# Second layer's Hadamard transform moved from TensorE to sums on GpSimd and VectorE

## The reference, cut to what matters

```python
def _ffn_ref(x, W1, W2, W3):                 # W1, W3: 1024 x 256, W2: 256 x 1024
    up_gate = jnp.einsum('bsd,hd->bsh', x, W1)
    up_lin = jnp.einsum('bsd,hd->bsh', x, W3)
    hidden = jax.nn.silu(up_gate) * up_lin
    hidden = fwht(hidden)                    # Walsh-Hadamard transform over 1024, times 1/sqrt(1024)
    out = jnp.einsum('bsh,dh->bsd', hidden, W2)
    return out

xn = _layernorm(x)
s, g = mixing(xn), silu(_ffn_ref(xn, W1, W2, W3))
x = x + s * g
```

## Time and profile before

| What | Value |
|---|---|
| median of 3 runs (lowest to highest) | 355.48 us (355.43 to 355.82) |
| time of the profiled execution | 355.68 us |
| its span | 353.6 us |
| TensorE busy | 347.7 us (98%) |
| VectorE busy | 249.3 us (71%) |
| ScalarE busy | 170.4 us (48%) |
| GpSimd busy | 109.7 us (31%) |
| DMA queue of SP, share of 16 engines | 37.9% |

### The profile page before, as it was taken

How to read it: one execution, slowest core, us unless ns; L and a number is a source line. 1 busy time by engine, 2 the same in 40 slices (tenths; PEclk the granted TensorE clock), 3 DMA queues, 4 the chain that set the end, 5 groups by cost and what they waited for, 6 DMA issues and landing times.

```text
span 353.6 us, 4944 instructions
## 1 busy us (share of the span) xinstructions
PE 347.7 (98%) x1760; PEld 295.6 (84%) x1760; DVE 249.3 (71%) x491; ACT 170.4 (48%) x335; POOL 109.7 (31%) x125
## 2 busy tenths in 40 slices
PE   7999999999999999999999999999999999999996
PEld 4888888888888888888987788888888888888896
DVE  5679973995489667966497956788657887367624
ACT  2865442446254724354466634654346544464531
POOL 2164410456026944663026030160300703004011
PEclk9999999999999999999999999999999999999999
DMA  7999479215141303130341401436014252064001
GB/s 262 239 186 214 111 142 154 61 44 126 50 111 29 121 1 118 32 121 0 115 142 41 123 0 59 142 80 198 3 50 149 72 135 74 0 193 129 7 0 61
DMA packets 70200, 34.44 MB, mean 97 GB/s; under 512 B 41248, under 2 KB 70176, under 8 KB 70176
## 3 DMA queue, kind: packets, MB, share of 16 engines
q1 hardware_dynamic: 69760, 33.80, 37.9%
q10 hardware_dynamic: 416, 0.33, 0.3%
HBM read 21.99 MB, written 12.12 MB: 96 GB/s over the span
## 4 chain that ended last, share of the span: by engine, by line
PE 90%; DVE 4%; POOL 2%; ACT 2%; DMA 1%; issue 1%; SPq 0%; DVEq 0%; POOLq 0%; ACTq 0%
PE GU L359 18%; PE GU L360 18%; PE GU L361 18%; PE O L359 8%; PE O L360 8%; PE O L361 8%; POOL X L1267 1%; PE O L420 1%; DMA X<-in_L_attn_x 1%; PE O L504 1%; PE O L503 1%; PE O L502 1%; PE T L361 1%; PE T L360 1%; PE T L359 1%; PE T L366 1%
## 5 line engine op out<-in xcount | busy, mean ns | idle before, releaser
L717 ACT ACTIVATE hf<-GU 128x512 f32<-128x512 f32 x64 | 38.2, 599 | 79.1 <-DVE hid L845 63.0
L1001 DVE TENSOR_TENSOR hf<-hf,GU 128x512 f32<-128x512 f32 x64 | 43.5, 680 | 27.7 <-PE GU L361 22.5
L359 PE MATMUL GU<-XT,W1T 128*128 128x512 f32 x128 | 50.5, 394 | 0.0
L845 DVE TENSOR_TENSOR hid<-hf,hid 128x512 fp32r<-128x512 f32 x64 | 50.0, 783 | 0.3
L359 PE MATMUL GU<-XT,W3T 128*128 128x512 f32 x128 | 49.9, 390 | 0.0
L361 PE MATMUL GU<-XT,W1T 128*128 128x512 f32 x128 | 49.9, 390 | 0.0
L360 PE MATMUL GU<-XT,W1T 128*128 128x512 f32 x128 | 49.9, 390 | 0.0
L361 PE MATMUL GU<-XT,W3T 128*128 128x512 f32 x128 | 49.8, 389 | 0.0
L360 PE MATMUL GU<-XT,W3T 128*128 128x512 f32 x128 | 49.8, 389 | 0.0
L360 PE MATMUL O<-hid,W2hi 128*128 128x512 f32 x112 | 43.7, 390 | 0.0
L359 PE MATMUL O<-hid,W2hi 128*128 128x512 f32 x112 | 43.7, 390 | 0.0
(11 more groups left out here) (200 smaller groups left out, 725.7 us busy)
## 6 DMA issues: line engine op xcount, KB each, us to landing
swap_rows<-GX SPq DMA_DIRECT2D x7, 512.0 KB, 3.1
sT<-swap_rows SPq DMA_DIRECT2D x28, 128.0 KB, 2.7
swap_gate<-GX SPq DMA_DIRECT2D x7, 512.0 KB, 2.9
sT<-swap_gate SPq DMA_DIRECT2D x28, 128.0 KB, 2.7
stage<-in_L_ffn_W SPq DMA_DIRECT2D x12, 256.0 KB, 3.9
swap_p<-PX SPq DMA_DIRECT2D x4, 640.0 KB, 3.7
PL<-swap_p SPq DMA_DIRECT2D x16, 160.0 KB, 3.2
stage<-in_L_ffn_W SPq DMA_DIRECT2D x32, 64.0 KB, 2.6
```

The lines of the kernel that those rows point to most:

```text
L359: pe.matmul(o, lhs(0), rhs(0), start=start, stop=False)
L717: act.activation(hf[:, c % 2, :], GU[:, c % 2, 0, :], ACT.Silu).then_inc(silu_done, 1)
L845: dve.tensor_tensor(dst, src, hi_part.bitcast(F32), ALU.subtract).then_inc(done, 1)
L1001: dve.tensor_tensor(hf[:, c % 2, :], hf[:, c % 2, :], GU[:, c % 2, 1, :], ALU.mult).then_inc(mul_done, 1)
```

## The change

The transform over the 128 positions of a chunk no longer uses TensorE. It is done in seven steps of sums and differences.

- Five steps on GpSimd, on the blocks as loaded and before they are transposed, where five of the seven bits of the position lie along the free dimension: `inner_butterfly(0)` to `(9)`, two instructions a step (all sums, then all differences), each with 1024 elements a partition in runs of 16, 8, 4, 2 and 1, between U2[1] and U[1]. Numbers 0 to 4 are in group 1 and 5 to 9 in group 2.
- `turn_w2` follows, all four in group 2 (two at c = 3, two at c = 7). `pair_butterfly` and `quad_butterfly` stand in groups 2 and 3, `last_butterfly` in group 3 and `w2_sums` in group 3 at c = 1.
- Two steps across partitions, after the transform over the 8 chunks. SP copies U2[1] to U[1] with its halves of 64 partitions exchanged (two DMAs of 512 KB), in group 3 between `spread_c2(0)` and the rows' scatter. VectorE adds, with a sign per partition from a column of the Hadamard matrix (`w2_cross(0, 0)` and `(0, 1)`, 128x1024 each, in group 4 after `x_lo`). SP then exchanges quarters of 32 partitions within each half (four DMAs of 256 KB) ahead of `move_gate(3)`, and VectorE adds again: `w2_cross(1, 0)` before the first chunk of group 4, `w2_cross(1, 1)` at its c = 3.

The factor 1/32 moves into `w2_hi` and `w2_lo`. The eight Hadamard passes, the hi and lo parts of w2nat and the four copies `pair_u` of the second layer are gone. The diff, without its unchanged lines:

```diff
...
-        w_turned, wx_hi, wx_lo, natx_hi, natx_ready = sem("w_turned"), sem("wx_hi"), sem("wx_lo"), sem("natx_hi"), sem("natx_ready")
+        w_turned, wx_hi, wx_lo = sem("w_turned"), sem("wx_hi"), sem("wx_lo")
...
-        w2_loaded, w2_turned = sem("w2_loaded"), sem("w2_turned")
+        w2_loaded, w2_turned, w2_inner, w2_swapped, w2_crossed = sem("w2_loaded"), sem("w2_turned"), sem("w2_inner"), sem("w2_swapped"), sem("w2_crossed")
...
+            def swap_partitions(width):
+
+                for p0 in range(0, P, width):
+                    sp.dma_start(U[1][p0:p0 + width, :, :], U2[1][p0 ^ width:(p0 ^ width) + width, :, :]).then_inc(w2_swapped, 16)
+
...
+                    sp.wait_ge(fly, 26)
+                    sp.wait_ge(fly_add, 2)
+                    swap_partitions(P // 2)
...
+            sp.wait_ge(w2_crossed, 2)
+            swap_partitions(P // 4)
...
-            def next_hadamard(i):
-
-                pe.wait_ge(u_ready, i - 1)
-                pe.wait_ge(natx_ready, i - PAIRS + 1)
-                pe.matmul(T[:, i % 2, :], hadmR[:, :], w2nat[:, 0, :, :].rearrange("p a d -> p (a d)"), start=True, stop=False)
-                pe.matmul(T[:, i % 2, :], hadmR[:, :], w2nat[:, 1, :, :].rearrange("p a d -> p (a d)"), start=False, stop=True).then_inc(h_done, 1)
-
...
-                    if c == 1 and n > 1:
-                        next_hadamard(PAIRS + 2 * n - 3)
-                if n == 1:
-                    pe.wait_ge(sm_lo, 3)
-                if n < 3:
-                    next_hadamard(PAIRS + 2 * n - 2)
...
-                    pe.wait_ge(u_ready, 2 * PAIRS)
+                    pe.wait_ge(sm_lo, 3)
...
-            def turned_nat_hi(i):
-
-                j = i - PAIRS
-                act.wait_ge(h_done, i)
-                hi(w2nat[:, 0, :, :], U2[1][:, 2 * j:2 * j + 2, :], w2_turned, j + 1, natx_hi)
-
...
-                bank = O[:, 1, :] if l == 0 else T[:, i % 2, :]
-                act.activation(U[l][:, 2 * j:2 * j + 2, :].rearrange("p a d -> p (a d)"), bank, ACT.Copy, scale=float(H) ** -0.5).then_inc(u_ready, 1)
+                act.activation(U[l][:, 2 * j:2 * j + 2, :].rearrange("p a d -> p (a d)"), O[:, 1, :], ACT.Copy, scale=float(H) ** -0.5).then_inc(u_ready, 1)
...
-                act.wait_ge(fly_add, l + 1)
-                act.wait_ge(fly, 13 * l + 13)
-                act.activation(W2hi[l][:, part, :], U2[l][:, part, :], ACT.Copy).then_inc(w2hi_ready, 1)
+                if l:
+                    act.wait_ge(w2_crossed, 3 + h)
+                else:
+                    act.wait_ge(fly_add, 1)
+                    act.wait_ge(fly, 13)
+                act.activation(W2hi[l][:, part, :], U2[l][:, part, :], ACT.Copy, scale=(1.0, float(H) ** -0.5)[l]).then_inc(w2hi_ready, 1)
...
-                    if c == 2 and n > 1:
-                        pair_u(1, PAIRS + 2 * n - 3, 2 * n - 3)
...
-                    if c == 4 and n < 3:
-                        turned_nat_hi(PAIRS + 2 * n - 2)
...
-                    pair_u(1, PAIRS + 2 * n - 2, 2 * n - 2)
-                    turned_nat_hi(PAIRS + 2 * n - 1)
...
-                lo(W2lo[l][:, part, :], U2[l][:, part, :], W2hi[l][:, part, :], w2hi_ready, 2 * l + h + 1, w2_ready)
+                if l == 0:
+                    lo(W2lo[l][:, part, :], U2[l][:, part, :], W2hi[l][:, part, :], w2hi_ready, h + 1, w2_ready)
+                else:
+                    dve.wait_ge(w2hi_ready, 2 + h + 1)
+                    dve.scalar_tensor_tensor(W2lo[1][:, part, :], U2[1][:, part, :], float(H) ** -0.5, W2hi[1][:, part, :].bitcast(F32),
+                                             ALU.mult, ALU.subtract).then_inc(w2_ready, 1)
+
+            def w2_cross(r, h):
+
+                part = slice(h * HC // 2, (h + 1) * HC // 2)
+                if h == 0:
+                    if r == 0:
+                        dve.wait_ge(hadm_loaded, 16)
+                    dve.wait_ge(w2_swapped, (32, 96)[r])
+                sign = hadm[:, (P // 2, P // 4)[r]:(P // 2, P // 4)[r] + 1]
+                dve.scalar_tensor_tensor(U2[1][:, part, :], U2[1][:, part, :], sign, U[1][:, part, :], ALU.mult, ALU.add).then_inc(w2_crossed, 1)
...
-                dve.wait_ge(w2_loaded, 16 * QUADS)
-                in_place(U2[1][:, 2 * j:2 * j + 2, :].rearrange("p c d -> p (c d)")).then_inc(w2_turned, 1)
+                dve.wait_ge(w2_inner, 10)
+                in_place(U[1][:, 2 * j:2 * j + 2, :].rearrange("p c d -> p (c d)")).then_inc(w2_turned, 1)
...
-                    if c == 3:
-                        turn_w2(2 * n - 2)
...
-                    if c == 7:
-                        turn_w2(2 * n - 1)
+                if n == 2 and c in (3, 7):
+                    for j in (c // 4 * 2, c // 4 * 2 + 1):
+                        turn_w2(j)
+                if n == 3 and c == 1:
+                    w2_sums(1)
+                if n == NB and c == 3:
+                    w2_cross(1, 1)
...
+                if prev_layer == 0:
+                    w2_cross(0, 0)
+                    w2_cross(0, 1)
...
+                if prev_layer == 0:
+                    w2_cross(1, 0)
...
-                    if prev_layer == 0 and c == 2:
-                        w2_sums(1)
...
-                pool.wait_ge(u_ready, u_value)
+                if l:
+                    pool.wait_ge(w2_turned, j + 1)
+                else:
+                    pool.wait_ge(u_ready, u_value)
...
+            def inner_butterfly(i):
+
+                if i == 0:
+                    pool.wait_ge(w2_loaded, 16 * QUADS)
+                elif i % 2 == 0:
+                    pool.wait_ge(w2_inner, i)
+                t, width = i // 2, Q >> (i // 2 + 1)
+                src, dst = (V[1][:, :, :].rearrange("p c d -> p (c d)").rearrange("p (g e w) -> p g e w", e=2, w=width)
+                            for V in ((U2, U), (U, U2))[t % 2])
+                pool.tensor_tensor(dst[:, :, i % 2, :], src[:, :, 0, :], src[:, :, 1, :], ALU.subtract if i % 2 else ALU.add).then_inc(w2_inner, 1)
+
...
-            def nat_lo(i):
-                j = i - PAIRS
-                pool.wait_ge(natx_hi, j + 1)
-                pool.tensor_tensor(w2nat[:, 1, :, :], U2[1][:, 2 * j:2 * j + 2, :], w2nat[:, 0, :, :].bitcast(F32), ALU.subtract).then_inc(natx_ready, 1)
-
...
-                if n > 1:
-                    nat_lo(PAIRS + 2 * n - 3)
-                    pair_butterfly(1, 2 * n - 4, PAIRS + 2 * n - 3)
+                if n == 1:
+                    inner_butterfly(0)
+                if n == 2:
+                    for i in range(5, 10):
+                        inner_butterfly(i)
+                if n == NB - 1:
+                    pair_butterfly(1, 2, 0)
+                    pair_butterfly(1, 3, 0)
+                    quad_butterfly(1, 0, 17)
+                    quad_butterfly(1, 1, 21)
...
+                if n == 1:
+                    inner_butterfly(1)
...
+                if n == 1:
+                    inner_butterfly(2)
...
-                    nat_lo(PAIRS + 2 * n - 2)
-                if n > 1:
-                    pair_butterfly(1, 2 * n - 3, PAIRS + 2 * n - 2)
-                    quad_butterfly(1, n - 2, (17, 23)[n - 2])
+                if n == 1:
+                    inner_butterfly(3)
+                    inner_butterfly(4)
+                if n == 2:
+                    pair_butterfly(1, 0, 0)
+                    pair_butterfly(1, 1, 0)
```

## The result

The change takes **364.8 us** (median of 5 runs, 363.49 to 365.69), against 355.68 us before in the same comparison (5 runs): ratio 1.0253, interval 1.0235 to 1.0272. The prediction was 364.0 us in 359 to 371. Its profiled execution took 365.69 us, with a span of 363.8, so 10.2 us more than the span before; the prediction's sum for a profiled execution was +8.5.

What follows compares the result with a forecast made beforehand. The prediction took TensorE, busy 98% of the 353.6 us span, to bound the kernel. Its terms, -1.81 + 1.05 + 0.42 + 4.05 + 0.74 + 3.4 + 0.66, summed to +8.5 us on the median 355.48: 364.0 us, range 359 to 371.

Steps and rivals of the forecast that it cites:

- What is removed, -1.81: Groups 1 to 3: two TensorE Hadamard passes fewer for each of four W2 pairs, 0.45 us a pair, -1.81 us.
- Sums of 2.40 us: GpSimd, groups 1 and 2: each of the ten 128x1024 sums takes 2.40 us, whatever its run length.
- The rival of slower narrow runs: GpSimd's ten sums: at 3.2 us each, +12.5 us, 368.0 us; at 3.9 us each, +19; chance 0.2.
- Group 1, +1.05: End of group 1: third sum delays chunk 3's lo part, so chunk 6's product reaches TensorE's recurrent mix late, +1.05 us.
- the down chunks, +0.42: Group 2's third down chunk waits for a lo part held up by sums four and five, +0.42 us.
- Start of group 2, +4.05: VectorE's two x_lo instructions wait for the seventh and eighth sums, so TensorE gets x late, +4.05 us.
- Group 3, +0.74: Start of group 3: x_lo meets two 1.25 us GpSimd pair or quad sums behind rms, +0.74 us.
- AR of group 4, +3.4: TensorE's wait for zT: x_turn 1.74 us late, row scatter 2.3 later behind the exchange, less 0.66 slack; +3.4 us.
- I take 4.2, nearer the gather: SP's queue before group 4: exchange of halves (1 MB) takes 4.2 us, between scatter-rate 3.0 and gather-rate 4.7.
- Group 4, +0.66: Chunks of group 4: third signed sum 0.4 us late before chunk 0, with the fourth +0.66; signed sums 1.2 us each.
- The clock: Rival: after each of two long waits, TensorE's first 12 matmuls run at 1.2 GHz, 2.7 us more each; chance 0.08.
- the port terms: Waits from the rule that two-SBUF-input VectorE instructions and large GpSimd ones exclude each other; largest +4.05 at group 2's start.

Runs made afterwards that it cites:

- e10: e9 with GpSimd's additions to X of groups 1 to 3 waiting for all four of VectorE's gate products; 353.79 us, ratio 0.9944.
- e3: The changed kernel without both exchanges of partitions (six DMAs), all sums and signed sums kept; 359.45 us, ratio 1.0104.
- e8: The changed kernel with each exchange DMA replaced by a straight copy of the same bytes over all 128 partitions; 361.33 us, ratio 1.0169.
- e2: The changed kernel without sums 2 to 9 of GpSimd's ten; 361.94 us, ratio 1.0164.
- e11: The kernel before the change, with only the edit that e10 has over e9; 355.63 us against 355.62, ratio 0.9998.
- e7: The changed kernel with 20 more matmuls of 512 columns, result unused, ahead of AR in group 4; 363.17 us, ratio 1.0214.
- e9: The changed kernel with sums, last subtraction and halves' exchange moved to places meant to make nothing wait, two such places then mended; 354.97 us, ratio 0.9985.

## Why the prediction was right, and where its terms were off

- **What is removed, -1.81.** Right: TensorE's starts give 0.45 to 0.47 us at each of the four places, and e10 reaches 353.79 us, 1.84 below the kernel before.
- **Sums of 2.40 us.** Nearly: those in runs of 16, 8 and 4 elements take 2.37 to 2.41 us alone. Those in runs of 2 and 1 take 1.90, below the end that I had called low ("no pattern has fewer elements"). The rival of slower narrow runs had the sign wrong.
- **Group 1, +1.05, and the down chunks, +0.42.** Mechanism right (the lo part of chunk 3 took 2.14 us beside the third sum), size too large: +0.3 and +0.2. The third sum started at 71.74, not 72.3, and the product of chunk 6 came at 79.0, not 79.7.
- **Start of group 2, +4.05.** Seventh and eighth sum, as forecast, but +2.5: rms ended 1.2 us earlier than I had it (88.98 against 90.2), as group 1 had lost less, and the seventh sum was one of the short ones.
- **Group 3, +0.74.** +0.2 measured; x_lo took 3.37 us there.
- **AR of group 4, +3.4.** The part without a transfer was exact: 1.08 forecast, 1.10 in e3. The term that was mis-sized is the exchange: "I take 4.2, nearer the gather". It lands 6.3 us after issue, the scatter behind it in 7.9 instead of 5.3, and SP is held for 1.34 us at the issue: in all 4.3 us at TensorE where I had 2.3. The nearest row was the gather's, 224 GB/s, and the quarters' exchange moved at just that rate (4.7 us for 1 MB); I had taken a price between it and the scatter's 350 GB/s. The Trainium skill (SBUF — State Buffer, "Door 1: The DMA port swizzle") says that half the partitions reach only half of the DMA ports. An estimate from its 196 GB/s is 5.3 us for the exchange and +4.5 us for this term, nearer to the +5.4 measured than mine. The traces agree in that the same bytes over all 128 partitions move 1.7 times as fast (e8, 381 against 224 GB/s); e8 doesn't separate the number of partitions from the rest of the exchange.
- **Group 4, +0.66.** +0.2: signed sums of 1.2 us were right (1.26), 1.75 beside the additions.
- **The clock.** A rival with 0.08, now part of what happens: +1.5 us behind AR, +1.7 behind the start of group 2 in some executions, against 2.7 each that I priced. My price took 12 matmuls; 7 to 9 ran slowly (in e2 it was 12, and they cost 2.5 us).

So 364.0 came near 364.8 by errors against each other, which is luck: the port terms were too large by 3.5 us in sum, the exchange too small by 2.0, and the clock's 3.2 was left to a rival. The places and their causes were right; the sizes were less good than the total looks.

## What to carry to other kernels

Moving work to an engine with free time is paid in waits, and the waits depend on where the work stands: the same instructions cost +9 us here in one order and gained 1.8 in another. Before a large GpSimd instruction is placed, look for VectorE's next work with two inputs in SBUF, and if TensorE waits for that work, hold GpSimd back by a semaphore until it is done, even if GpSimd stands idle meanwhile; where TensorE doesn't wait, this gives nothing (e11). Put a bulk transfer behind the small one that the next stage waits for, and expect an exchange between parts of the partitions to move more slowly than a copy over all 128 (224 against 381 GB/s here).

## What the runs showed of the hardware

- Sums over 128x1024 with both inputs in runs of 1 or 2 elements take 1.90 us on GpSimd, those in longer runs 2.37 to 2.41.
- After a wait of 5.25 us TensorE ran at half clock for 7 matmuls (1.5 us lost), after 5.72 us (e2) for 12 (2.5 us lost). After a wait of 2.3 to 2.4 us it did so in some executions (clock 0.995, +1.7 us) and not in others (1.000).
- With matmuls in the wait, those behind it ran at full clock (e7).
- VectorE's gate products took 2.51 to 2.53 us beside GpSimd's additions and 1.42 to 1.43 us ahead of them (e9 and e10, the kernel before and e11).
- A 512 KB scatter issued behind the two 512 KB DMAs of the exchange held its queue for 1.34 us at issue. Behind two straight copies of the same size (e8) it took 0.37, behind nothing 0.36.
